# A recommender's session stage: the second product made while rows are read in, and a table with copies of its last row

## What is computed

```
h = emb; acc = emb                                      # 12501 x 128
repeat twice: h = segment_sum(adj_val * h[adj_col], adj_row); acc = acc + h
graph = acc / 3
combined = graph[items] + item_features[items]          # items: 512 sessions x 50
seq = take_along_axis(combined, alias_inputs)           # 512 x 50 x 128
mask = inputs != 0
hs = sum(seq * mask) / sum(mask)                        # mean of a session, 512 x 128
nh = tanh(concat([flip(emb[:50]), seq]) @ w_1)
nh = sigmoid(nh @ glu1_w.T + glu1_b + (hs @ glu2_w.T)[:, None, :])
beta = nh @ w_2 * mask
select = 12 * l2norm(sum(beta * seq))                   # 512 x 128
scores = select @ l2norm(graph).T                       # 512 x 12501
```

## Time and profile before

| | us |
|---|---|
| median of 3 runs | 4142.29 (4141.05 to 4148.06) |
| profiled execution: its own time | 4142.95 |
| profiled execution: span from first to last instruction | 4141.2 |
| the table is complete, the first session gather is issued | 3757.5 |
| second product of step 0, 1, 2, 3 begins | 3831.7, 3898.1, 3982.0, 4061.6 |
| scores of step 4 begin | 4112.3 |

### The profile page before, as it was taken

One profiled execution on the slowest core, in us unless ns is written; L12 is line 12 of the kernel. 1 busy time (PEld: TensorE's weight loads), 2 busy tenths in 40 slices (PEclk: granted clock), 3 DMA queues, 4 the chain that ended last, 5 costly groups with the idle time before them and its releaser, 6 DMA issues. The chain is left out here.

```text
span 4141.2 us, 69284 instructions
## 1 busy us (share of the span) xinstructions
PE 3114.1 (75%) x10054; PEld 1840.1 (44%) x10054; DVE 3033.3 (73%) x7214; ACT 877.0 (21%) x3009; POOL 2871.6 (69%) x2965
## 2 busy tenths in 40 slices
PE   6999995777777777777776777777777777776878
PEld 5777774333333333333333334333344433433444
DVE  8999995777777777777775776776767767776655
ACT  3999996000000000000001000000000000007443
POOL 1677766777777777777775777777777777775750
PEclk8899987777777777777776776776777777666889
DMA  1000000222222222222225222222222222247993
GB/s 36 4 3 3 3 3 23 56 55 55 55 55 55 55 55 55 55 55 55 55 54 161 56 55 55 55 55 55 55 55 55 55 55 55 55 115 98 70 114 157
DMA packets 162231, 235.38 MB, mean 57 GB/s; under 512 B 67554, under 2 KB 107776, under 8 KB 161952
## 3 DMA queue, kind: packets, MB, share of 16 engines
q0 software_dynamic: 92896, 171.14, 21.5%
q1 hardware_dynamic: 54132, 58.90, 4.4%
q10 hardware_dynamic: 15052, 3.83, 0.6%
HBM read 192.69 MB, written 41.01 MB: 56 GB/s over the span
## 5 line engine op out<-in xcount | busy, mean ns | idle before, releaser
L1456 PE MATMUL bank<-ring 128*128 128x256 f32 x4976 | 2168.1, 570 | 822.8 <-DVE ring L1117 795.3
L1456 PEld LDWEIGHTS bank<-ring 128*128 128x128 f32 x4976 | 1130.2, 264 | 1835.1 <-DVE ring L1117 1768.4
L1117 DVE TENSOR_SCALAR ring<-bank,mlo,mval 128x256 f32<-128x256 f32 x2488 | 1343.8, 540 | 710.5 <-DMA ring<-table,cring 356.8
L580 POOL DMA_INDIRECT ring<-table,cring x1195 | 1127.6, 944 | 397.0 <-issue 352.3
L580 POOL DMA_INDIRECT ring<-in_L_rec_emb,cring x1195 | 1131.7, 947 | 368.8 <-issue 355.6
L1166 DVE TENSOR_TENSOR acc<-acc,bank 128x256 f32 x2488 | 1019.2, 410 | 140.9 <-issue 140.0
L656 ACT ACTIVATE big<-big 128x68 f32<-128x68 bf16 x1764 | 557.4, 406 | 0.0
L1376 PE MATMUL bank<-big,ring 128*128 128x136 f32 x2352 | 438.8, 323 | 63.1 <-DVE ring L884 17.8
L549 POOL DMA_INDIRECT sorted_edges<-moved,block_to x313 | 397.2, 1269 | 101.3 <-issue 101.3
L1376 PEld LDWEIGHTS bank<-big,ring 128*128 128x128 f32 x2352 | 344.4, 210 | 151.6 <-ACT big L656 132.6
L672 ACT COPY mlo<-ring 128x24 f32 (+1 forms) x104 | 21.9, 211 | 1553.2 <-PE bank L1456 1519.3
(11 more groups left out here) (214 smaller groups left out, 1659.2 us busy)
## 6 DMA issues: line engine op xcount, KB each, us to landing
ring<-in_L_rec_emb SPq DMA_DIRECT2D x3136, 0.5 KB
ring<-in_L_rec_emb ACTq DMA_DIRECT2D x3136, 0.5 KB
ring<-table ACTq DMA_DIRECT2D x3136, 0.5 KB
ring<-table SPq DMA_DIRECT2D x3136, 0.5 KB
scores<-stage SPq DMA_DIRECT2D x48, 512.0 KB, 3.0
ring<-in_L_rec_emb,cring POOLq DMA_INDIRECT x1195, 3.7
ring<-table,cring POOLq DMA_INDIRECT x1195, 3.8
table<-big SPq DMA_DIRECT2D x7, 896.0 KB, 8.7
```

What stands on the lines that cost most here:

```text
L580: pool.indirect_dma_start(msg[:, s, :], None, source, bass.IndirectOffsetOnAxis(cring[:, s:s + 1], 0)).then_inc(s_g[s], 16)
L1117: dve.tensor_scalar(onehot[:, u % SR, :], bank[7][:, 0:BUCKET], mlo[:, u:u + 1], mval[:, u:u + 1], ALU.is_equal, ALU.mult).then_inc(s_S[u ...
L1456: pe.matmul(bank[u % PR][:, 0:BUCKET], msg[:, h * T + u, :], onehot[:, u % SR, :], start=True, stop=True).then_inc(s_mm[u % M], 1)
```

## The change

The clamp of the row number no longer has one upper bound but one for each partition, `own_last` = 12500 + p, and the table has 127 more rows with copies of its last row. The row that a session takes where its item is too large is then that of its partition. The last transfer of the table is cut in three: 13 whole blocks, the 85 rows of the last block, and one transfer that writes row 12500 once more to 127 rows, out of one SBUF partition. POOL and DVE wait for nine transfers and no longer for seven.

The second product is made as a group is read in, one group behind the first product. ACT copies it into `nh1`, over the tanh vectors that it was made from (`keep_product`). As the mean isn't known then, DVE adds `bias2` in the read-out step, now from SBUF (`nh1`) and no longer from PSUM. The read-in of block 0 has one PSUM bank for each step, as that of the others. ACT's copy of a table of column numbers signals another semaphore; this changes no work.

```diff
-        combined = nc.dram_tensor("combined", [ROWS, D], F32).ap()
+        combined = nc.dram_tensor("combined", [N + COPIES, D], F32).ap()
...
+                if b <= emb_full:
+                    sp.dma_start(tab[1][:, a:b, :], ring_rows[:, a:b, :]).then_inc(s_cw, 16)
+                    continue
+                sp.dma_start(tab[1][:, a:emb_full, :], ring_rows[:, a:emb_full, :]).then_inc(s_cw, 16)
+                sp.dma_start(tab[1][0:emb_rest, emb_full, :], ring_rows[0:emb_rest, emb_full, :]).then_inc(s_cw, 16)
+                sp.dma_start(combined[N:N + COPIES, :].rearrange("(o n) d -> o n d", o=1),
+                             ring_rows[emb_rest - 1:emb_rest, emb_full, :].unsqueeze(1).broadcast_to([1, COPIES, D])
+                             ).then_inc(s_cw, 16)
...
-            pool.wait_ge(s_cw, 16 * (NB // GRP))
+            pool.wait_ge(s_cw, 16 * (NB // GRP + 2))
...
+            def keep_product(bt, k):
+                m, n = NG * bt + k, min(LG, L - LG * k) * P
+                act.wait_ge(s_y, m + 1)
+                act.copy(nh1[:, k * LG * P:k * LG * P + n], bank[2 + m % 2][:, 0:n]).then_inc(s_ye, 1)
...
-                if k:
+                if 0 < k <= NG:
                     tanh_step(bt, k - 1)
+                if k > 1:
+                    keep_product(bt, k - 2)
...
-                link(dve.tensor_scalar(it_n[:, :, :], it_f[:, :, :], 0.0, float(N - 1), ALU.max, ALU.min))
+                link(dve.tensor_scalar(it_n[:, :, :], it_f[:, :, :], own_last[:, 0:1], 0.0, ALU.min, ALU.max))
...
-                        dve.wait_ge(s_y, m + 1)
+                        dve.wait_ge(s_ye, m + 1)
...
-                                          bank[2 + m % 2][:, 0:n * P].rearrange("p (l n) -> p l n", n=P),
+                                          nh1[:, k * LG * P:(k * LG + n) * P].rearrange("p (l n) -> p l n", n=P),
...
+            def second_product(bt, k):
+                m, n = NG * bt + k, min(LG, L - LG * k) * P
+                pe.wait_ge(s_th, m + 1)
+                ge(pe, s_ye, m - 1)
+                pe.matmul(bank[2 + m % 2][:, 0:n], g1T[:, :], nh1[:, k * LG * P:k * LG * P + n],
+                          start=True, stop=True).then_inc(s_y, 1)
...
-                        pe.wait_ge(s_th, m + 1)
-                        ge(pe, s_ya, m - 1)
-                        pe.matmul(bank[2 + m % 2][:, 0:n], g1T[:, :], nh1[:, k * LG * P:k * LG * P + n],
-                                  start=True, stop=True).then_inc(s_y, 1)
                     rows_in(w + 1, k)
...
                     scores(w - 1, 2 * k)
                     if k and w + 1 < BT:
                         first_product(w + 1, k - 1)
+                    if k > 1 and w + 1 < BT:
+                        second_product(w + 1, k - 2)
                     scores(w - 1, 2 * k + 1)
                 if w + 1 < BT:
                     first_product(w + 1, NG - 1)
+                    second_product(w + 1, NG - 2)
+                    second_product(w + 1, NG - 1)
                 if w < BT:
                     read_out(w, NG - 1)
```

More of the change, by code:

```diff
@@ L93, in recommender_program @@
     OPEN, NORMS = 5, 8
+    COPIES = P - 1
     assert NST // 2 - 1 == L // 2 and HALF % AT_ONCE == 0 and NST % 2 == 0
@@ L248, in recommender_program @@
         startc = sb("startc", [P, 1])
+        own_last = sb("own_last", [P, 1])
         tile_off = sb("tile_off", [1, NT], I32)
@@ L288, in recommender_program @@
         row_c = bank[1][:, 0:LC]
-        def in_bank(bt, k, q):
-            return bank[q + (2 * (k % 2) if bt == 0 else 0)]
         def fours(b):
@@ L389, in recommender_program @@
         s_y = sem("s_y")
+        s_ye = sem("s_ye")
         s_ya = sem("s_ya")
@@ L412, in recommender_program @@
         emb_rest = N - emb_full * P
-        tab = [t.rearrange("(g p) d -> p g d", p=P) for t in (table1, combined)]
+        tab = [t[0:ROWS, :].rearrange("(g p) d -> p g d", p=P) for t in (table1, combined)]
+        assert N + COPIES >= ROWS and emb_full == ROWS // P - 1 and 0 < emb_rest < P
         big_rows = big[:, :].rearrange("p (g d) -> p g d", d=D)
@@ L560, in _ @@
                       allow_small_or_imprecise_dtypes=True).then_inc(s_lat, 1)
-            pool.wait_ge(s_lat, 2)
+            pool.iota(own_last[:, :], [[0, 1]], base=N - 1, channel_multiplier=1,
+                      allow_small_or_imprecise_dtypes=True).then_inc(s_lat, 1)
+            pool.wait_ge(s_lat, 3)
             pool.memset(block_id_l[0:1, 0:SKIPL], FAR).then_inc(s_lat, 1)
@@ L677, in _ @@
             act.activation(acc[:, :], ones[:, 0:1].broadcast_to([P, ROWS]), ACT.Copy, scale=0.0).then_inc(s_az, 1)
-            act.copy(bank[7][:, 0:BUCKET], iota_r[:, :]).then_inc(s_iota, 1)
+            act.copy(bank[7][:, 0:BUCKET], iota_r[:, :]).then_inc(s_az, 1)
             for m in range(-(-NT // P)):
@@ L762, in tanh_step @@
                 act.wait_ge(s_z, m + 1)
-                ge(act, s_y, NG * (bt - 1) + k + 1)
+                ge(act, s_ya, NG * (bt - 1) + k + 1)
                 for j in range(w):
                     l = LG * k + j
-                    last = act.activation(nh1[:, l * P:(l + 1) * P], in_bank(bt, k, 1)[:, j * P:(j + 1) * P],
+                    last = act.activation(nh1[:, l * P:(l + 1) * P], bank[1][:, j * P:(j + 1) * P],
                                           ACT.Tanh, bias=posb[:, L - 1 - l:L - l])
                 last.then_inc(s_th, 1)
+            def keep_product(bt, k):
+                m, n = NG * bt + k, min(LG, L - LG * k) * P
+                act.wait_ge(s_y, m + 1)
+                act.copy(nh1[:, k * LG * P:k * LG * P + n], bank[2 + m % 2][:, 0:n]).then_inc(s_ye, 1)
             def read_in(bt, k):
@@ L777, in read_in @@
                     ge(act, s_z, m - 1)
-                    act.copy(xT[:, m % 2, 0:w * P], in_bank(bt, k, 0)[:, 0:w * P]).then_inc(s_xc, 1)
-                if k:
+                    act.copy(xT[:, m % 2, 0:w * P], bank[0][:, 0:w * P]).then_inc(s_xc, 1)
+                if 0 < k <= NG:
                     tanh_step(bt, k - 1)
-            for k in range(NG + 1):
+                if k > 1:
+                    keep_product(bt, k - 2)
+            for k in range(NG + 2):
                 read_in(0, k)
@@ L800, in _ @@
                 read_in(w + 1, NG)
+                read_in(w + 1, NG + 1)
                 if w < BT:
@@ L1071, in _ @@
             sort_group(GR - 2, 1, LCL)
-            dve.wait_ge(s_lat, 3)
+            dve.wait_ge(s_lat, 4)
             dve.wait_ge(s_rk, RANK * GR)
@@ L1177, in _ @@
             dve.sem_inc(s_acc[M - 1], 1)
-            dve.wait_ge(s_az, 3)
-            dve.wait_ge(s_iota, 1)
+            dve.wait_ge(s_az, 4)
             dve.wait_ge(s_toff, 3)
@@ L1499, in first_product @@
                 pe.wait_ge(s_xc, m + 1)
-                ge(pe, s_th, m if bt else m - 1)
-                pe.matmul(in_bank(bt, k, 1)[:, 0:w * P], w1b[:, :], xT[:, m % 2, 0:w * P], start=True, stop=True).then_inc(s_z, 1)
+                ge(pe, s_th, m)
+                pe.matmul(bank[1][:, 0:w * P], w1b[:, :], xT[:, m % 2, 0:w * P], start=True, stop=True).then_inc(s_z, 1)
+            def second_product(bt, k):
[4 more added lines that the diff above has]
+                          start=True, stop=True).then_inc(s_y, 1)
             def rows_in(bt, k):
@@ L1508, in rows_in @@
                 pe.wait_ge(s_sq[bt % 2 * NG + k], 16 * (LAYERS * FED[bt % 2 * NG + k] + w * (bt // 2 + 1)))
-                ge(pe, s_xc, m if bt else m - 1)
+                ge(pe, s_xc, m)
                 for j in range(w):
-                    last = pe.transpose(in_bank(bt, k, 0)[:, j * P:(j + 1) * P], seq[:, bt % 2, LG * k + j, :], ident[:, :])
+                    last = pe.transpose(bank[0][:, j * P:(j + 1) * P], seq[:, bt % 2, LG * k + j, :], ident[:, :])
                 last.then_inc(s_x, 1)
@@ L1533, in scores @@
                           start=True, stop=True).then_inc(s_sc, 1)
-            for k in range(NG):
-                rows_in(0, k)
-                if k:
+            for k in range(NG + 2):
+                if k < NG:
+                    rows_in(0, k)
+                if 0 < k <= NG:
                     first_product(0, k - 1)
-            first_product(0, NG - 1)
+                if k > 1:
+                    second_product(0, k - 2)
             for w in range(BT + 1):
@@ L1550, in _ @@
                     if w < BT:
-                        m, n = NG * w + k, min(LG, L - LG * k) * P
-                        if k == 0 and w == 0:
-                            pe.wait_ge(s_th, NG)
                         if k == 1:
```

4 lines of the change are left out of this document (1 added, 3 removed).

## The result

The changed kernel takes 4108.30 us in the median (4106.67 to 4108.77), the kernel before 4144.59 beside it: a ratio of 0.9912, with a 95% interval of 0.9895 to 0.9929. The profiled execution of the changed kernel has a time of 4108.61 us and a span of 4106.8, before 4142.95 and 4141.2. So 34 to 36 us were gained where 44.9 were forecast; 4108 lies inside the range of 4086 to 4119.

A forecast was written before the change was run, and what follows sets the result against it. Four bounds in turn: table writes, POOL's pace until step 1, DMA engines in steps 1 and 2, PE in step 3. Terms -1.4 - 28.7 - 0.9 - 4.2 - 9.7 = -44.9 took 4142.95 to 4098 us; range 4086 to 4119.

The forecast's parts named there:

- The full engines, -28.7: Steps 1 and 2: stalls above 67.4 us vanish as gather packets fall from 0.58 to 0.135 us: 16.5 + 12.2.
- The table's start, +3.9: Table's last transfers: 127 copies go to one DMA engine, so POOL's first session gather moves from 3757.5 to 3761.4.
- Up to the first scores of step 1, -2.8: From DVE's first row of `combined`: 31.4 + 137.3 us forecast, 27.5 + 144.0 before; gathers land after 3.8 us.
- DVE's add against POOL's issues: Read-out: 39 adds now reading SBUF twice could slow POOL's gather issues by some tenths of a us.
- the tail from first product 11 to read out 12: End of steps 1 and 2 on PE: 2.85 us grows to 3.7 with more products there, +0.85.
- The starts of steps 1, 2 and 3, -4.2: Read out 12 to first scores falls from 6.84 to 5.4 us without the second product ahead of the session vector.
- The order on PE, -0.9: Steps 1 and 2: turn 1 loses 0.86, turn 12 loses 0.43, the tail gains 0.85; -0.44 each.
- ACT's copies, 0: 52 new copies of 0.57 us on ACT, 3.5 us busy in a 4.77 us turn: hidden by PE, cost 0.
- Rivals 2 and 4: Steps 1, 2: ACT's copy exposed, +12.5, 4110.5 (11%); or ACT and PE in series, 6.9 a turn, 4158 (2%).
- Step 3, -9.7: Step 3, no gathers: turns of 3.46 us lose the 0.94 second product, less 0.13 for handovers: 12 x 0.81.

The follow-up runs named there:

- four_rows: The changed kernel with the clamp using 4 copies of the last row instead of 127, all 127 still written: 4111.93 us.
- two_rows: The changed kernel with the clamp using 2 copies of the last row instead of 127, all 127 still written: 4110.03 us.
- table_only: The kernel before with only the table's copies and the clamp by partition, second product left where it was: 4116.83 us, ratio 0.9942.
- before_again: The kernel before, unedited, in a second profiled execution: 4132.43 us, 401.9 us from DVE's first row of `combined` where the first profile had 411.2.
- copies128: The changed kernel with 128 copies of the last row instead of 127, the 128th read by nobody: 4108.61 us, ratio 0.9922.
- warm: The changed kernel with products on PE that nobody reads, put into its waits at the starts of steps 1 to 4: 4100.75 us, ratio 0.9903.
- table_warm: The kernel before with the table's part alone, plus unread products on PE at the starts of steps 1 to 4: 4108.91 us, ratio 0.9919.

## Why the prediction was right, and where its sum was off

The sum of stages was 366.4 us from DVE's first row, and 376.3 came out. By its steps:

- **The full engines, -28.7: right in cause and place.** The share fell to 0.19 (0.25 was named), turns of steps 1 and 2 are 4.72 us (4.77), DVE's and ACT's waits for the scores' transfers are gone, and the last gather is issued at 4016.6 (4013) with 0.6 us of waits for places in all. four_rows and two_rows show that it was the repetition of the row. Against before's own profile steps 1 and 2 gained 15.7 and 11.0 us. table_only, which has this part alone, gained 17.0 and 13.3 there, 30.3 us together. What I didn't see is that the 0.58 us were those of one execution: against before_again table_only gained 10.1 and 16.7, together 26.8, and step 0 was 5.8 us shorter there without any change. The sum of this term holds against either; that it fell so close in each step is the luck of the one execution.
- **The table's start, +3.9: 3.1 measured, for the most part for another reason.** That the copies go to one engine is worth 1.1 us, where the whole 3.9 was put down to it. The two further transfers, which I had put at nothing, are 2.0. The closeness of the sum is luck.
- **Up to the first scores of step 1, -2.8 in all with that start: -1.1 measured.** The landing is better than assumed (2.6 for 3.8 us), but two terms were too small. DVE's add against POOL's issues was put at some tenths and costs 2.3 to 2.9 us up to the 100th issue. And the tail from first product 11 to read out 12 grew from 2.85 to 4.27 us (+1.42), where I had +0.85; 0.46 of it is PE's wait for a tanh of ACT's (timeline of after, end of step 2):

```profile
4030.34 0.67 PE L1516 MATMUL bank<-big,w1b 128*128 128x256 f32 x2 [0.46 <-ACT big L773]
```

- **The starts of steps 1, 2 and 3, -4.2: the step that failed.** I counted from read out 12 to the first scores and expected 5.4 us; that part holds with 5.07. But I ended the count at the first scores and took the turn behind them from before, with before's clock in it. From them to read out 1 it is now 10.30 us (3900.88 to 3911.18), and was 7.69 (3901.51 to 3909.20 in before), because the turn now runs at the granted clock of 0.50 all through: +2.6 in the turn, against the 2.2 that this start gained (7.26 to 5.07). In after step 1 is 68.2 us and step 2 68.2 where 65.6 and 65.1 were forecast. Where the lower level was over after 3.4 us, the same path takes 7.37 us (3903.00 to 3910.37 in copies128), and the steps come to 66.3, 65.3 and 65.8. So the misses of these two steps are those of the long stretches. That they agree to a tenth with the 5.6 us which after pays for the clock against warm is chance, for the forecast itself had before's clock in it (2.7 us by table_only less table_warm). And with the clock held, where products that nobody reads stand in the waits of either order, the move doesn't give the 1.4 a start: steps 1 and 2 are then the same with both.
- **The order on PE, -0.9, and ACT's copies, 0:** the tail's further 0.57 us stand at the end of steps 1 and 2 too, so nothing is left of the -0.9. Beyond that there is no trace of a cost: warm's steps 1 and 2 together differ by 0.7 us from table_warm, without the moved product. Rivals 2 and 4 are out: no turn of steps 1 and 2 shows ACT as the one that PE's scores wait for.
- **Step 3, -9.7: right at the higher clock, 7.0 as it ran.** Its turns take 2.61 us, where 2.6 to 2.7 was expected (timeline of after):

```profile
4049.03 0.95 PE L1541 MATMUL bank<-w2c,big 128*128 128x1 f32 x8
...
4051.64 0.95 PE L1541 MATMUL bank<-w2c,big 128*128 128x1 f32 x8
```

  The 10 us at 0.51 from 4037 on take the rest; with warm's products step 3 is 36.1 us, 10.2 less than in table_warm.

So the misses are -0.8 at the table, +2.5 in step 0, +2.6, +3.1 and +2.7 in steps 1 to 3 and -0.2 at the end, +9.9 together. The clock at the starts is worth more than the 8.4 of steps 1 to 3: with warm's products they take 166.9 us, 10.3 less than in after, where 168.8 were forecast with before's clock in them. What stays open is what sets the length of the lower level, 3.4 or 10 us in the same code and some 7 at two starts of before: warm shows that it doesn't come when PE is given work in the waits, not what ends it.

## What to carry to other kernels

Before a full DMA queue is put down to traffic, compare the time of a packet with that of the same transfer elsewhere in the trace: here the repetition of one row within a gather made it more than four times as long in one execution and 1.8 times in another, and two rows in place of the one nearly cure it. Where the work around an engine's wait is changed, count past the end of the wait for as long as the clock stays low: here that was mostly 10 us, with full turns in them, and unread products in the wait took 8 to 12 us back. And hold a change against more than one profile of the kernel before, if something in it is full to the brim.

## What the runs showed of the hardware

Gathers in which some 94 of 128 rows are the same HBM row kept the 16 DMA engines at 0.91 in one execution of a kernel and at 0.37 in another, both at 53 GB/s; spread over two rows they took 0.23, over four 0.18. An indirect transfer's issue on POOL, 0.94 us by itself, grew up to 1.61 us where DVE's add of 128x512 with both inputs in SBUF overlapped it. Two further small transfers of the table cost 2.0 us together, in whichever order they were issued, and 127 rows out of one partition 1.1 us more than 128. TensorE fell to 0.50 of its clock at each start of a step in after, in the first of them after an idle stretch of 2.06 us and 1.0 us of work, as PE went idle for another 0.83, and stayed there for 10 us in which PE was busy for 9.2 to 9.7. In other executions of the same session code it was back at 1.00 after 3.4 us, and with products in the waits it never fell there.
